# A recurrence with its chunks on the free axis, and the same with chunks on partitions and two steps per transpose

## The reference

```python
O_lh, O_rh = polar_orthogonal(W_lh), polar_orthogonal(W_rh)   # 12 iterations X = 1.5 X - 0.5 X X' X
q, v = xn @ Wq.T, xn @ Wv.T
h = identity                                                  # for each of the 8 sequences
for t in range(512):
    h = rms(h @ O_lh.T + q[t] @ O_rh.T)                       # rms(z) = z / sqrt(mean(z*z) + 1e-6)
    qs[t] = h
out = x + (qs * v) @ Wc.T + sqrt((xn @ cos(theta + theta_noise))**2 + (xn @ sin(phi + phi_noise))**2)
```

## Time and profile before

| | us |
|---|---|
| median of 3 runs | 170.09 |
| lowest and highest run | 169.50 and 170.56 |
| span of the profiled execution | 168.3 |
| polar iterations and layernorm | up to about 31 |
| recurrence with its side work | 33.9 to 159 |
| rest | 159 to 168.3 |

### The profile page before, as it was taken

How to read it: one execution, slowest core, us unless ns; L and a number is a source line. 1 busy time by engine, 2 the same in 40 slices (tenths; PEclk the granted TensorE clock), 3 DMA queues, 4 the chain that set the end, 5 groups by cost and what they waited for, 6 DMA issues and landing times.

```text
span 168.3 us, 3931 instructions
## 1 busy us (share of the span) xinstructions
PE 149.2 (89%) x1068; PEld 126.7 (75%) x1068; DVE 130.5 (78%) x549; ACT 116.7 (69%) x482; POOL 103.3 (61%) x241
## 2 busy tenths in 40 slices
PE   6888888789999999999879999999599999999900
PEld 6866777478888888987667777777498888889800
DVE  6599998498888999998987777777946666666860
ACT  3147999957766889999767777777557677676600
POOL 7007777123443477899837777777659787877700
PEclk9999999999999999999999999999969999999985
DMA  4880000000000000000000000000000003030330
GB/s 100 240 300 1 4 2 0 0 4 2 0 0 6 0 0 4 4 0 0 2 6 0 0 0 0 6 2 0 0 0 6 0 0 127 6 125 0 125 125 10
DMA packets 3497, 5.06 MB, mean 30 GB/s; under 512 B 464, under 2 KB 1616, under 8 KB 3472
## 3 DMA queue, kind: packets, MB, share of 16 engines
q1 hardware_dynamic: 3168, 4.46, 8.5%
q0 software_dynamic: 160, 0.26, 0.5%
q10 hardware_dynamic: 144, 0.07, 0.1%
HBM read 2.69 MB, written 2.10 MB: 28 GB/s over the span
## 4 chain that ended last, share of the span: by engine, by line
PE 56%; DVE 31%; issue 7%; ACT 3%; DVEq 0%
PE bank L869 16%; PE bank L856 14%; DVE MIX L698 9%; PE bank L867 6%; PE bank L835 4%; DVE FS L664 4%; DVE WT L705 4%; PE bank L821 3%; PE bank L776 3%; PE bank L762 2%; DVE EDGE_RI L607 2%; DVE PXT L566 2%; PE bank L753 2%; PE bank L727 2%; ACT RT L447 2%
## 5 line engine op out<-in xcount | busy, mean ns | idle before, releaser
L350 POOL TENSOR_TENSOR Q<-RT 128x128 bf16<-128x128 f32 (+1 forms) x108 | 50.8, 471 | 40.5 <-ACT RT L447 39.5
L698 DVE TENSOR_TENSOR MIX<-UT,RT 128x128 f32<-128x128 f32 x108 | 39.2, 363 | 19.3 <-ACT RT L447 15.4
L856 PE MATMUL bank<-WT,PXT 128*128 128x128 f32 x212 | 48.4, 310 | 4.1 <-DVE WT L694 3.5
L447 ACT ACTIVATE RT<-bank 128x128 f32<-128x128 f32 x108 | 29.9, 277 | 23.9 <-PE bank L869 23.0
L869 PE MATMUL bank<-SQ,MEAN 128*128 128x128 f32 (+1 forms) x180 | 41.9, 292 | 0.4
L856 PEld LDWEIGHTS bank<-WT,PXT 128*128 128x128 f32 x212 | 32.1, 191 | 10.0 <-DVE WT L694 4.3
L441 ACT ACTIVATE SQ<-WT 128x128 f32<-128x128 f32 (+1 forms) x106 | 32.5, 307 | 6.3 <-DVE WT L694 2.9
L869 PEld LDWEIGHTS bank<-SQ,MEAN 128*128 128x128 f32 (+1 forms) x180 | 24.6, 165 | 11.1 <-ACT SQ L441 9.2
L705 DVE TENSOR_TENSOR WT<-MIX,bank 128x128 f32<-128x128 f32 x102 | 28.4, 278 | 4.6 <-DVE MIX L698 0.5
L867 PE MATMUL bank<-Q,EPS_MEAN 128*128 128x128 bf16 (+1 forms) x140 | 29.4, 245 | 0.0
L821 PE MATMUL bank<-CS,XNT 128*128 128x128 f32 x128 | 25.4, 280 | 0.0
(11 more groups left out here) (132 smaller groups left out, 235.4 us busy)
## 6 DMA issues: line engine op xcount, KB each, us to landing
X<-in_L_attn_x_dram SPq DMA_DIRECT2D x8, 256.0 KB, 6.1
out_dram<-OUT SPq DMA_DIRECT2D x6, 256.0 KB, 2.8
out_dram<-OUT SPq DMA_DIRECT2D x4, 128.0 KB, 2.1
WP<-in_L_attn_W_rh_dram ACTq DMA_DIRECT2D x1, 64.0 KB, 2.0
WP<-in_L_attn_W_lh_dram SPq DMA_DIRECT2D x1, 64.0 KB, 2.2
ANG<-in_L_ffn_theta_dram POOLq DMA_DIRECT2D x1, 64.0 KB, 4.2
WV<-in_L_attn_Wv_dram SPq DMA_DIRECT2D x1, 64.0 KB, 4.0
ANG<-in_L_ffn_phi_dram POOLq DMA_DIRECT2D x1, 64.0 KB, 4.0
```

The lines of the kernel that those rows point to most:

```text
L350: pool.tensor_tensor(split((Q16 if guess(at) else Q)[g][:, :]), r, r, ALU.mult).then_inc(q_ready[g], 1)
L447: act.activation(r_of(j, g), split(SUM[g][:, 0:P]), ACT.Sqrt).then_inc(r_ready[g], 1)
L698: dve.tensor_tensor(split(MIX[g][:, :]), split(UT[:, cols(j, g)]), r_before(j, g), ALU.mult).then_inc(m_ready[g], 1)
L856: pe.matmul(split(Y[g][:, 0:P]), OT[0][:, :], w, start=True, stop=True).then_inc(y_ready[g], 1)
```

## The change

The recurrence is turned around. A state now has its 128 chunks on partitions and its channels on the free axis, so the sum of squares of a chunk is accumulated by the instruction that squares it, and the norm is one number per partition.

- A column of constant `EPS_COL` = sqrt(eps C) stands beside each input tile (`UZ`, width 129 used of 130), so that the sum of squares holds eps. The Q products, the matmuls with `MEAN` and `EPS_MEAN`, and the bf16 copies go.
- Each new state must be transposed for the next product: PE transposes W into `TY`, DVE copies it to `WT`. At the end of a pass the transpose is a product with `DIAG` = identity over the norm, and the copy goes to `EDGE`, shifted by one chunk.
- In the guess passes a move takes two steps: from the same transposed state PE computes Y = O W and TY = O^2 W. DVE makes the middle state `WMID` (needed only for its norm), its sum of squares (`tensor_tensor_reduce`), adds r0 Z in PSUM and then r_mid U. Z is a second input, with N = O M.
- O^2 and N are computed once: `OL` (O as it is), `O2T`, `M`, `MNT`, with the order of the two last polar products swapped.
- `FIRST` is 5, and there are three guess passes and the last one; the last takes single steps. That is 42 slots of two steps and 32 of one.
- Feed-forward work is done once per tile of 128 channels instead of in two halves, its sum moves from DVE to POOL, both groups in one instruction (256 wide). The row factors need no packing any more.
- The test compares the ends of the last guess pass and the last pass.

The core of the diff, shortened:

```diff
-FIRST = 6
-WARM = 4
+FIRST = 5
+GUESS_PASSES = 3
...
+    MOVES = [(j + 1, 0, 2, False) for j in range(FIRST + 1, STEPS, 2)]
+    for p in range(1, GUESS_PASSES):
+        MOVES += [(j + 1, p, 2, j == 0) for j in range(0, STEPS, 2)]
+    TWOS = len(MOVES)
+    MOVES += [(j, GUESS_PASSES, 1, j == 0) for j in range(STEPS)]
...
+    FFN0 = 12
+    FFN_SLOTS = {}
+    for h in range(TILES):
+        FFN_SLOTS.setdefault(FFN0 + (h // 2 if h < 4 else h - 2), []).append(h)
+    V_SLOTS = {FFN0 + 1 + i * 28 // 15: i for i in range(2 * BATCHES)}
...
 # POOL
+            def ffn_sum(f):
+                pool.wait_ge(S["ffn_sq"], f + 1)
...
+                pool.tensor_tensor(FS[:, f % 2, :, :], FSQ[:, f % 2, :, 0:P], FSQ[:, f % 2, :, P:2 * P],
+                                   ALU.add).then_inc(S["ffn_sum"], 1)
+            def ffn_added(f):
+                pool.wait_ge(S["ffn_root"], f + 1)
+                pool.tensor_tensor(XF[:, :, f, :], X[:, :, f, :], FR[:, f % 2, :, :],
+                                   ALU.add).then_inc(S["xf_done"], 1)
...
 # ACT
             act.activation(ROOT_OF_ONE[:, 1:2], ONES[:, 0:1], ACT.Sqrt)
+            act.wait_ge(S["ol_done"], 1)
+            act.copy(OL[:, :], NEXT[0][:, 0:P]).then_inc(S["ol_copied"], 1)
+            act.wait_ge(S["m_done"], 1)
+            act.copy(M[:, :], GRAM[1][:, 0:P]).then_inc(S["m_copied"], 1)
+            act.wait_ge(S["o2_done"], 1)
+            act.copy(O2T[:, :], NEXT[1][:, 0:P]).then_inc(S["o2_copied"], 1)
+            xt_copied(BATCHES - 1)
...
+                act.activation(SQE[:, 0:E], state(s, g)[:, 0:E], ACT.Square,
+                               accum_out=SSE[:, g:g + 1]).then_inc(ss_ready[g], 1)
+                act.wait_ge(ss_ready[g], s + 1)
+                act.activation(RT[:, t:t + 1], SSE[:, g:g + 1], ACT.Sqrt, scale=1.0 / C).then_inc(r_ready[g], 1)
...
+            for n in range(SLOTS):
+                m, g = divmod(n, GROUPS)
+                if m < TWOS:
+                    act.wait_ge(ssm_ready[g], m + 1)
+                    act.activation(RM[:, g:g + 1], SSM[:, g:g + 1], ACT.Sqrt, scale=1.0 / C).then_inc(rm_ready[g], 1)
+                if 0 <= n - 1 < len(LATE):
+                    pair_copied(NEARLY + n - 1)
+                for h in FFN_SLOTS.get(n - 1, ()):
+                    if h % 2:
+                        ffn_squared(h // 2)
+                for h in FFN_SLOTS.get(n - 3, ()):
+                    if h % 2:
+                        ffn_root(h // 2)
+                if V_SLOTS.get(n - 1, 0) % 2:
+                    v_copied(V_SLOTS[n - 1] // 2)
+                norm_of_state(m + 1, g)
...
 # DVE
+            def end_scaled(s, g):
+                t = tile(state_step(s), g)
+                dve.wait_ge(r_ready[g], s + 1)
+                dve.reciprocal(EINV[:, g:g + 1], RT[:, t:t + 1]).then_inc(einv_ready[g], 1)
+                dve.wait_ge(einv_ready[g], bounds_before(s) + 1)
+                dve.tensor_scalar(DIAG[g][:, :], IDENT[:, :], EINV[:, g:g + 1], None,
+                                  ALU.mult).then_inc(diag_ready[g], 1)
...
+            def two_steps(n, m, g, j):
+                r0 = norm_of(m, g)
...
+                dve.scalar_tensor_tensor(out=WMID[g][:, 0:E], in0=UZ[:, uz(j - 1, g), 0:E], scalar=r0,
+                                         in1=Y[g][:, 0:E], op0=ALU.mult, op1=ALU.add).then_inc(mid_ready[g], 1)
+                dve.wait_ge(mid_ready[g], m + 1)
+                dve.tensor_tensor_reduce(out=SQM[:, 0:E], in0=WMID[g][:, 0:E], in1=WMID[g][:, 0:E], scale=1.0,
+                                         scalar=0.0, op0=ALU.mult, op1=ALU.add,
+                                         accum_out=SSM[:, g:g + 1]).then_inc(ssm_ready[g], 1)
+                prev, po = divmod(n - 1, GROUPS)
+                if n == 0 or ends_pass(prev + 1):
+                    if n:
+                        end_scaled(prev + 1, po)
+                    else:
+                        transposed(0, 1)
+                else:
+                    transposed(prev + 1, po)
+                dve.wait_ge(y2_done[g], m + 1)
+                dve.scalar_tensor_tensor(out=TY[g][:, 0:P], in0=UZ[:, uz(j - 1, g) + 1, 0:P], scalar=r0,
+                                         in1=TY[g][:, 0:P], op0=ALU.mult, op1=ALU.add).then_inc(pre_ready[g], 1)
+                dve.wait_ge(pre_ready[g], m + 1)
+                dve.wait_ge(rm_ready[g], m + 1)
+                dve.scalar_tensor_tensor(out=W[g][:, 0:E], in0=UZ[:, uz(j, g), 0:E], scalar=RM[:, g:g + 1],
+                                         in1=TY[g][:, 0:E], op0=ALU.mult, op1=ALU.add).then_inc(w_ready[g], 1)
+                if n and ends_pass(prev + 1):
+                    transposed(prev + 1, po)
...
+            def one_step(n, m, g, j):
...
+                dve.scalar_tensor_tensor(out=W[g][:, 0:E], in0=UZ[:, uz(j, g), 0:E], scalar=norm_of(m, g),
+                                         in1=Y[g][:, 0:E], op0=ALU.mult, op1=ALU.add).then_inc(w_ready[g], 1)
...
+                transposed(prev + 1, po)
...
 # PE
+            pe.matmul(NEXT[0][:, 0:P], PXT[(POLAR_ITERS - 1) % 2][0][:, :], PP[0][:, :], start=True,
+                      stop=True).then_inc(S["ol_done"], 1)
+            pe.wait_ge(pxt_copied[1], POLAR_ITERS + 1)
+            pe.matmul(GRAM[0][:, 0:P], WQ[:, :], OT[1][:, :], start=True, stop=True).then_inc(S["mt_done"], 1)
+            pe.matmul(GRAM[1][:, 0:P], OT[1][:, :], WQ[:, :], start=True, stop=True).then_inc(S["m_done"], 1)
+            pe.wait_ge(pxt_copied[0], POLAR_ITERS + 1)
+            pe.wait_ge(S["ol_copied"], 1)
+            pe.matmul(NEXT[1][:, 0:P], OL[:, :], OT[0][:, :], start=True, stop=True).then_inc(S["o2_done"], 1)
+            pe.wait_ge(S["mt_copied"], 1)
...
+            transposed(0, 0)
+            transposed(0, 1)
+            for i in range(NEARLY):
+                pair(i)
+            for n in range(SLOTS + 2):
+                m, g = divmod(n, GROUPS)
+                prev, po = divmod(n - 1, GROUPS)
+                if n < SLOTS:
+                    steps = MOVES[m][2]
+                    pe.wait_ge(wt_ready[g], m + 1)
+                    pe.matmul(Y[g][:, 0:P], stationary(m, g), OT[0][:, :], start=True, stop=True).then_inc(y1_done[g], 1)
+                    if steps == 2:
+                        pe.matmul(TY[g][:, 0:P], stationary(m, g), O2T[:, :], start=True,
+                                  stop=True).then_inc(y2_done[g], 1)
+                if 0 < n <= SLOTS:
+                    transposed(prev + 1, po)
+                if n < len(LATE):
+                    pair(NEARLY + n)
+                for h in FFN_SLOTS.get(n, ()):
+                    ffn(h)
+                if n in V_SLOTS:
+                    values(V_SLOTS[n])
+                if 0 <= n - 2 - OUT0 < TILES:
+                    projected(n - 2 - OUT0)
```

More of the change, by code:

```diff
@@ L249, in ffn_item @@
-        def ffn_item(slot, again):
-            k = slot - TILES
-            return k if 0 <= k < FFN_PASSES * TILES and not again else None
-        def out_item(slot, again):
-            m = slot - OUT_AT
-            return (m, again * TILES + m) if 0 <= m < TILES else (None, None)
-        def batch(m, again):
-            b, i, n = BATCH_OF[m]
-            return again * len(OUT_BATCHES) + b, i, n
-        OUT_TILES = {}
-        for first, size in OUT_BATCHES:
-            for i in range(size):
-                ready = first + size - 1 + 5
-                OUT_TILES.setdefault(ready + (i if ready < TILES else i // 2), []).append(first + i)
@@ new lines, in inverse, with written @@
+            def inverse(t):
+                j, g = divmod(t, GROUPS)
+                dve.wait_ge(r_ready[g], TWOS + j + 2)
+                dve.reciprocal(RINV[:, t:t + 1], RT[:, t:t + 1]).then_inc(S["rinv_done"], 1)
+            def written(t):
+                j, g = divmod(t, GROUPS)
+                dve.wait_ge(S["xf_done"], j + 1)
+                dve.wait_ge(S["rinv_done"], t + 1)
+                dve.wait_ge(S["y_done"], t + 1)
+                dve.scalar_tensor_tensor(out=OUT[:, g, j, :], in0=OUT_BANKS[t % 4][:, 0:P], scalar=RINV[:, t:t + 1],
+                                         in1=XF[:, g, j, :], op0=ALU.mult, op1=ALU.add).then_inc(S["out_done"], 1)
@@ new lines, in _ @@
+            for g in range(GROUPS):
+                dve.wait_ge(t_done[g], LAST + 2)
+                dve.tensor_copy(edge_new(EDGE[g][CHECK % 2]), ends(TY[g][:, 0:P])).then_inc(S["edges"], 1)
+            for g in range(GROUPS):
+                dve.wait_ge(S["edges"], g + 1)
+                dve.tensor_tensor(DIFF[:, g, :], edge(EDGE[g][CHECK % 2]),
+                                  edge(EDGE[g][(CHECK + 1) % 2]), ALU.subtract).then_inc(S["diff_done"], 1)
+            dve.wait_ge(S["diff_done"], GROUPS)
@@ L722, in _ @@
+            further_passes(dve, again)
         @block.tensor
@@ L726, in keep_warm @@
                 for _ in range(n):
[L727 removed]
```

(11 more changed lines are left out.)

750 lines of the change are left out of this document (339 added, 411 removed).

## The result

| us | before | after |
|---|---|---|
| median | 170.32 | 178.58 |
| lowest to highest of four runs each | 169.50 to 170.58 | 177.08 to 178.86 |
| span of the profiled execution | 168.3 | 176.8 |
| first instruction of the first slot | 33.9 | 40.99 |
| start of the last W | | 164.56 |

The change makes the kernel slower: the ratio is 1.048, interval 1.043 to 1.053. I had predicted 163.6 and faster. Against my sum of 161.8 us for the span, 15.0 us are missing.

What follows compares the result with a forecast made beforehand. Bound: latency of a ring crossing four engines, not one engine's work. Span 39.2+0.7+64.3+7.4+4.6+34.7+5.85+5.05 = 161.8 us, plus 1.8 to the median of runs: 163.6 us, 3.8% faster, range 158 to 172.

Steps and rivals of the forecast that it cites:

- the last pass priced at full clock: Last pass, one-step slots: 1.12 us each, 31 x 1.12 = 34.7 us to the start of the last W.
- Clock rival: Last pass: granted clock falls throughout, Y takes 0.68 instead of 0.49, 6.1 us more, 169.7 us; chance 0.15.
- The two-step slot: Guess passes: 1.53 us a slot for two steps, 42 x 1.53 = 64.3 us.
- The accumulator read: Two-step slot: counted as occupying DVE, putting the copy's end at 0.67 rather than 0.60.
- Side work: The 30 feed-forward slots: POOL adds, V on PE and ACT copies cost 3.5, 0.8 and 0.3, together 4.6 us.
- the pass changes: Three changes, each in two slots of 2.69 us, adding 7.4 us.
- The dear-DVE rival: Two-step slots: five DVE instructions cost 0.20 us more together, 8.4 us in all, 172.0 us; chance 0.11.
- POOL and DVE: Feed-forward slots: half the reduces meet a POOL add and are held, 15 x 0.23 = 3.5 us.
- The upper bound: Feed-forward slots: each POOL add could hold a reduce for most of its length, 30 x 0.33 = 9.9 us.
- The start: Before the first slot: first WMID at 39.2 us, plus 0.7 for a lower clock (0 to 1.3).
- The wait on OL: Before the first slot: PE waits for ACT's OL copy, done at 33.8 us, and all else queues behind PE.
- The end: After the last W starts: DIAG at 2.43, flag at 5.85 us, then 5.05 to the end of the span.

Runs made afterwards that it cites:

- The third run: The changed kernel with idle products on PE only around the last pass change, none in the slots of the last pass; 168.01 us.
- the earlier start: The changed kernel with the copies of OL, M, O2T and the first four pairs made by DVE instead of ACT; 177.61 us.

## Why the prediction was wrong, by its own steps

**The step that failed: the last pass priced at full clock, with the Clock rival at 0.15 and its price too low.** My sum has 31 x 1.12 = 34.7 us for that pass, 36.3 with its part of the pass change; it took 49.0, and both signs that I had named for it (a last pass slower than 1.3, a clock under 1.00) came. I had the rival in words ("for the whole pass") and gave it 0.15 because "a slower PE is a busier one" and "it came back". In the earlier trace rows it came back in a loop with four products a slot; here it doesn't, in a loop with two products and a transpose. The argument should have been turned round: the new last pass has less on PE than the old one, so what brought the clock back there may be missing. The runs with added products show that this was so. The price was mis-sized too. The 0.68 of the earlier trace rows is a matmul that straddles the fall; whole at the lower level it is 0.80, so a slot loses 0.31, not 0.19. With 28 slots and the stall it is 9.1 us, and by 0.31 x 32 = 9.9 on top of 163.6 the rival would have read 173.5.

**The last pass at full clock: 1.20, not 1.12.** The third run shows it: W to copy 0.27, Y at 0.60, its end at 1.09, W at 1.20. Up to there I am 0.01 off. The hand-over from PE to the W instruction is 0.11, where I took the 0.03 between PE and ACT of the earlier trace rows. 30 slots x 0.08 = 2.4 us. With the stall I hadn't seen (2.29 there, 1.1 over a slot), one slot of 1.56 (0.4) and a pass change that was 0.2 shorter (2.47) it makes the 3.6 us that aren't the clock's: 12.7 = 9.1 + 3.6.

**The two-step slot was right within 0.04; that the whole stage is off by only 0.1 us is luck, since three errors cancel.** The first slots:

```profile
40.99 0.35 DVE L626 SCALAR_TENSOR_TENSOR WMID<-UZ,RT,bank 128x129 f32<-128x129 f32 x1 [3.54 <-PE bank L872]
...
41.38 0.29 DVE L629 CUSTOM_DVE_ANT_0 SQM<-WMID 128x129 f32<-128x129 f32 x1
41.60 0.08 DVE L629 DVE_READ_ACCUMULATOR2_ANT SSM<- 128x1 f32 x1
41.60 0.29 DVE L607 COPY WT<-bank 128x128 f32<-128x128 f32 x1
...
41.94 0.49 PE L872 MATMUL bank<-PXT,WT 128*128 128x128 f32 x2 [0.22 <-DVE WT L607]
...
42.56 0.35 DVE L626 SCALAR_TENSOR_TENSOR WMID<-UZ,RT,bank 128x129 f32<-128x129 f32 x1
```

The accumulator read starts together with the copy, so it costs nothing (-0.07); the hand-over from PE is 0.13 (+0.10): 1.57 against 1.53, 42 x 0.04 = 1.7 us more. Side work was less: passes two and three have 28 slots outside their changes, and took 23.0 + 22.7 us against 28 x 1.57 = 44.0, so 1.7 us for what I priced at 4.6, 2.9 less. And the pass changes were 1.2 us dearer up to the first W of the last pass: 5.5, 6.0 and 3.3 us for the first, the second and the first half of the third, against 2.69 a slot. The dear-DVE rival is out.

**POOL and DVE.** The mechanism was right, the size wasn't:

```profile
73.80 0.73 POOL L298 TENSOR_TENSOR FS<-FSQ 128x256 f32<-128x256 f32 x1 [1.79 <-ACT FSQ L412]
...
74.27 0.40 DVE L629 CUSTOM_DVE_ANT_0 SQM<-WMID 128x129 f32<-128x129 f32 x1
```

Its group on the page (count, busy us, mean ns):

```profile
L629 DVE CUSTOM_DVE_ANT_0 SQM<-WMID 128x129 f32<-128x129 f32 x42 | 13.9, 330 | 1.4
```

13 of the 42 reduces met such an add, in every other slot as I had it, and took 0.40 to 0.42 instead of 0.29; the mean over all 42 is 330 ns, so 42 x 0.04 = 1.7 us in all against my 3.5. The reduce ends at 74.67, 0.14 behind the add's end at 74.53, as in the earlier trace rows, and it is short only because it starts late in the add. The Trainium skill, SBUF — State Buffer, Who interferes with whom, calls the shared port pair an exclusive lock. The 13 reduces agree: each ends 0.14 to 0.16 behind the end of its add. The upper bound that I hung on it is far from the 1.7 us, since the starts decide how much of an add a reduce meets. Three scalings at the pass changes met an add too: DIAG took 0.55, 0.55 and 0.43 instead of 0.29; the first two are 0.5 us of the 1.2 above.

**The start: +1.1.** The wait on OL was right in place and size, PE idling for it, at the lower clock behind:

```profile
33.79 0.25 ACT L379 COPY OL<-bank 128x128 f32<-128x128 f32 x1
...
34.18 0.59 PE L796 MATMUL bank<-PXT,OL 128*128 128x128 f32 x2 [1.73 <-ACT OL L379]
```

I took 0.7 for the clock and bounded it by 1.3; the clock was 0.57 from 34 to 38 us. The run with 1.00 there had its first WMID at 39.08, where I had 39.2 for that case. So the route was right and the term is 1.9 (3.0 where the clock was 0.50 throughout).

**The end: +1.3.** DIAG starts 2.40 after the last W, where I had 2.43, but that match is luck: it is at the lower clock, and where the clock stayed at 1.00 behind the last W it is 2.10. From there to the flag's end it takes 4.9, not 3.4: the second group's DIAG and edge copy come 0.66 behind the first's, and the matmul over 256 columns keeps DVE idle for 1.31. In the run with idle products in the slots only, the clock was 1.00 up to about 163 us; there the two parts are 2.10 and 4.5, and that idle time 1.01. So of the 7.3 us from the last W to the flag's end, where I had 5.85, the clock has 0.7 and my sum left out the other 0.7. From flag to end it is 4.9, where I had 5.05.

## What to carry to other kernels

When a change takes work off TensorE in a loop that TensorE's latency paces, price the loop at both clock levels, with a matmul that ran wholly at the lower one, and ask of each thin stretch ahead of the loop whether the loop would bring the clock back; that it came back in the old kernel says nothing of the new. Here twenty idle products at one pass change, half of them in waits that existed anyway, were worth 9 us, while those put in front of queued work at the other two cost 1.3 us. For a ring of short instructions take each hand-over from a pair of the same engines and the same kind of instruction.

## What the runs showed of the hardware

- The granted clock has a memory: the same loop ran at 1.00 (1.20 us a slot, for 30 us and more) and at 0.50 (1.51, for over 40 us), by what came ahead of it.
- A 128-column float32 matmul on an idle PE takes 0.49 us at 1.00 and 0.80 at 0.50.
- Whether the clock fell at the second pass change differed between kernels with the same code there (84 to 88 us: 1.00 in the changed kernel, 0.50 from 86 to 88 with the earlier start), and from 34 to 38 us it was 0.50, 0.57 or 1.00 with the same code. What decides it stays open.
- A scalar_tensor_tensor that waits for PE starts 0.11 to 0.13 us after the matmul's shown end, a copy (of EDGE, at 117.10 in the changed kernel) 0.04 us after it.
